# Expert FFN in one kernel: the first bank of block 0 by samples, other filler counts, block 0's second weight asked for by GpSimd, and block 1's order of work

## The reference

```
h = gelu(x @ Wi[e] + bi[e])            # 256 -> 1024, erf form
r = h @ Wo[e] + bo[e] + x              # 1024 -> 256
y = (r - mean(r)) * rsqrt(var(r) + 1e-12) * gamma[e] + beta[e]
```

## Time and profile before

| | us |
|---|---|
| median of 3 runs | 121.52 (121.5 to 121.61) |
| the profiled execution, its own time | 122.44 |
| its span, first to last instruction | 120.7 |
| TensorE busy in the span | 111.6 |
| DVE, ScalarE, GpSimd busy | 97.9, 94.6, 56.1 |
| mean granted TensorE clock | 0.974 |

### The profile page before, as it was taken

One profiled execution on the slowest core, in us unless ns is written; L12 is line 12 of the kernel. 1 busy time (PEld: TensorE's weight loads), 2 busy tenths in 40 slices (PEclk: granted clock), 3 DMA queues, 4 the chain that ended last, 5 costly groups with the idle time before them and its releaser, 6 DMA issues.

```text
span 120.7 us, 2768 instructions
## 1 busy us (share of the span) xinstructions
PE 111.6 (92%) x886; PEld 109.4 (91%) x886; DVE 97.9 (81%) x192; ACT 94.6 (78%) x187; POOL 56.1 (47%) x84
## 2 busy tenths in 40 slices
PE   5959999999999999999999999999999999999900
PEld 5848999999999999999999999999999999999800
DVE  2563079995979999999999999999999994975660
ACT  2261799798899999999999999999989929972100
POOL 5035001803647464652846375374724880493420
PEclk9995999999999999999999999999999999999995
DMA  2989999999999989987998899999930140011032
GB/s 63 291 265 326 349 395 395 387 400 392 383 384 376 360 268 328 379 271 200 375 380 234 268 329 312 234 356 312 309 132 5 46 120 16 3 49 43 11 81 57
DMA packets 21400, 29.82 MB, mean 247 GB/s; under 512 B 2368, under 2 KB 11584, under 8 KB 21376
## 3 DMA queue, kind: packets, MB, share of 16 engines
q1 hardware_dynamic: 19008, 24.89, 61.4%
q0 software_dynamic: 864, 2.36, 6.2%
q10 hardware_dynamic: 1504, 2.30, 6.0%
HBM read 27.19 MB, written 2.36 MB: 245 GB/s over the span
## 4 chain that ended last, share of the span: by engine, by line
PE 74%; DMA 9%; SPq 4%; DVE 4%; issue 3%; POOL 2%; ACT 0%; POOLq 0%; DVEq 0%
PE preact L834 12%; PE sums_ps L867 12%; PE preact L808 11%; PE preact L807 11%; PE sums_ps L808 11%; PE sums_ps L807 11%; DMA params<-vectors 7%; SPq L271 3%; PE preact L831 3%; DMA xT_in<-x_columns 2%; PE preact L787 2%; DVE h_lo L684 1%; POOL rstd L428 1%; DVE r L692 1%; POOL xs L418 1%
## 5 line engine op out<-in xcount | busy, mean ns | idle before, releaser
L834 PE MATMUL preact<-xT_r,wi_lo 128*128 128x256 f32 x140 | 40.0, 286 | 0.0
L807 PE MATMUL preact<-xT_r,wi_hi 128*128 128x256 f32 x140 | 39.5, 282 | 0.0
L808 PE MATMUL preact<-xT_r,wi_hi 128*128 128x256 f32 x140 | 39.4, 281 | 0.0
L867 PE MATMUL sums_ps<-wo_r,h_lo 128*128 128x256 f32 x136 | 38.6, 284 | 0.2 <-DVE h_lo L684 0.2
L807 PE MATMUL sums_ps<-wo_r,h_hi 128*128 128x256 f32 x136 | 38.3, 282 | 0.0
L808 PE MATMUL sums_ps<-wo_r,h_hi 128*128 128x256 f32 x136 | 38.2, 281 | 0.0
L283 POOL DMA_INDIRECT xs<-x_rows,row_of x18 | 19.9, 1107 | 18.9 <-DMA wi_in<-w_in 9.7
L834 PEld LDWEIGHTS preact<-xT_r,wi_lo 128*128 128x128 f32 x140 | 26.5, 189 | 0.1
L807 PEld LDWEIGHTS preact<-xT_r,wi_hi 128*128 128x128 f32 x140 | 26.5, 189 | 0.1
L808 PEld LDWEIGHTS preact<-xT_r,wi_hi 128*128 128x128 f32 x140 | 26.4, 188 | 0.0
L684 DVE TENSOR_TENSOR h_lo<-preact,h_hi 128x512 fp32r<-128x512 f32 x34 | 23.3, 686 | 3.8 <-ACT h_hi L538 3.7
(11 more groups left out here) (70 smaller groups left out, 107.5 us busy)
## 6 DMA issues: line engine op xcount, KB each, us to landing
wo_in<-w_out SPq DMA_DIRECT2D x8, 1024.0 KB
wi_in<-w_in SPq DMA_DIRECT2D x7, 1024.0 KB, 7.1
params<-vectors SPq DMA_DIRECT2D x9, 388.0 KB
y_rows<-xs SPq DMA_DIRECT2D x35, 64.0 KB
xT_in<-x_columns SPq DMA_DIRECT2D x34, 64.0 KB, 4.5
wi_in<-w_in ACTq DMA_DIRECT2D x2, 512.0 KB, 4.4
wo_in<-w_out ACTq DMA_DIRECT2D x2, 512.0 KB, 5.6
wi_in<-w_in SPq DMA_DIRECT2D x2, 512.0 KB, 7.0
```

The source lines that it names most:

```text
L807: nc.tensor.matmul(columns, weight, parts[:, 0, :], start=False, stop=False)
L808: return nc.tensor.matmul(columns, weight, parts[:, 1, :], start=False, stop=stop)
L834: nc.tensor.matmul(columns, wi_lo[:, t % 2, c, k, :], xT_r[:, t % 2, k, 0, :], start=(k == 0), stop=False)
L867: nc.tensor.matmul(columns, h_lo[:, t % 2, c, tokens], wo_r[:, t % 2, c, 0, :], start=(c == 0), stop=False)
```

## The change

- `WARM_UP` becomes (4, 6, 1), and one filler of 32 columns follows the first four.
- Two semaphores `first_x_loaded` take samples 0 and 2 of block 0's x apart from 1 and 3. Bank 0 of block 0's first product is computed for samples 0 and 2 first, then for 1 and 3: 128 columns at a time, in eight matmuls instead of four.
- Block 0's second weight is asked for by GpSimd, right after its constants, and no longer by ScalarE.
- DVE writes the rest of the table and the row numbers after `x_low(0)`, no longer before `wi_low(0, 0)`.
- GpSimd gathers block 0's rows once `wi_loaded[2]` is there, and block 1's once `wo_loaded[1]` is there. Before, the first went out as soon as the row numbers stood, the second after `wi_loaded[2]`.
- In iteration 1, ScalarE does `gelu` and `h_high` of bank 0 before `wo_high(1, 0)`, and bank 1's before `wo_high(1, 1)`; DVE likewise; DVE's `centre(0, 0)` and `centre(0, 1)` stand one place later; ScalarE's `deviations` of block 0 and GpSimd's `root(0, 0)` move to iteration 2; GpSimd's first residual waits for `wo_low(1, 0)` alone.
- A store's wait for `y_ready` is part of the transfer's instruction.

```diff
...
     WO_PIECES = [(0, IC // 2), (IC // 2, SPLIT_CHUNKS)]
-    WARM_UP = (5, 4, 2)
+    WARM_UP = (4, 6, 1)
...
         par_loaded = [sem(f"par_loaded{i}") for i in range(PAR_RING)]
+        first_x_loaded = [sem(f"first_x_loaded{i}") for i in range(2)]
         xT_loaded = [sem(f"xT_loaded{i}") for i in range(XT_RING)]
...
                               xt[bass.ds(rows[j], 1), :, :].rearrange("o p f -> (o p) f")).then_inc(
-                                  xT_loaded[t % XT_RING], 16)
+                                  first_x_loaded[j % 2] if t == 0 else xT_loaded[t % XT_RING], 16)
...
             for j in slots:
-                eng.wait_ge(y_ready, 2 * t + j // 2 + 1)
-                eng.dma_start(out[bass.ds(rows[j], 1), :, :].rearrange("o s h -> (o s) h"), slot(t, j)).then_inc(
-                    stored[t % X_RING], 16)
+                eng.dma_start(out[bass.ds(rows[j], 1), :, :].rearrange("o s h -> (o s) h"), slot(t, j)).wait_op(
+                    y_ready, 2 * t + j // 2 + 1, "sem-ge").then_inc(stored[t % X_RING], 16)
...
+            for i, (a, z) in enumerate([(0, IC // 2), (IC // 2, IC)]):
+                pool.dma_start(wo_in[:, 0, a:z, :].rearrange("p c h -> p (c h)"), wo[0, :, a * H:z * H],
+                               max_dma_last_dim=PIECE).then_inc(first_wo_loaded[i], 16)
             def residual(t, tile):
...
                 if t == 1:
+                    pool.wait_ge(wo_lo_done[0], 1)
+                    residual(0, 0)
                     pool.wait_ge(wo_lo_done[1], wo_lo_count(1, 1))
-                    residual(0, 0)
                     residual(0, 1)
-                    root(0, 0)
                 else:
+                    if t == 2:
+                        root(0, 0)
                     if ahead:
...
             pool.wait_ge(rows_ready, 2)
+            pool.wait_ge(wi_loaded[2], 16)
             load_x(pool, 0)
-            pool.wait_ge(wi_loaded[2], 16)
+            pool.wait_ge(wo_loaded[1], 16)
             load_x(pool, 1)
...
             load_xT(act, 0, (2, 3))
-            for i, (a, z) in enumerate([(0, IC // 2), (IC // 2, IC)]):
-                act.dma_start(wo_in[:, 0, a:z, :].rearrange("p c h -> p (c h)"), wo[0, :, a * H:z * H],
-                              max_dma_last_dim=PIECE).then_inc(first_wo_loaded[i], 16)
...
             def x_high(t):
-                act.wait_ge(xT_loaded[t % XT_RING], 4 * loads_of(t, XT_RING))
+                if t == 0:
+                    for pair in range(2):
+                        act.wait_ge(first_x_loaded[pair], 16 * QUAD // 2)
+                else:
+                    act.wait_ge(xT_loaded[t % XT_RING], 4 * (loads_of(t, XT_RING) - (16 if t % XT_RING == 0 else 0)))
                 if t >= 2:
...
                     wi_high(2, 1)
-                    wo_high(1, 0)
-                    wo_high(1, 1)
                     gelu(1, 0)
                     h_high(1, 0)
+                    wo_high(1, 0)
                     gelu(1, 1)
                     h_high(1, 1)
+                    wo_high(1, 1)
                     gelu(1, 2)
                     h_high(1, 2)
-                    deviations(0, 0)
                     gelu(1, 3)
                     h_high(1, 3)
-                    deviations(0, 1)
                     return
...
                     wi_high(t + 1, 0)
+                    if t == 2:
+                        deviations(0, 0)
                     x_high(t + 1)
+                    if t == 2:
+                        deviations(0, 1)
                 gelu(t, 0)
...
                                           slot_of[:, 0:1], None, ALU.is_equal))
-            dve.wait_ge(permuted, 2)
-            nc.vector.tensor_tensor(table[:, FIRST:T_ALL], later_ps[0:1, FIRST:T_ALL], table_base[:, FIRST:T_ALL],
-                                    ALU.add).then_inc(table_ready, 1)
-            dve.wait_ge(const_step, 9)
-            dve.wait_ge(spread, 1)
-            for half in range(2):
-                rows = slice(half * S, (half + 1) * S)
-                nc.vector.scalar_tensor_tensor(row_of[rows, :], tab_ps[rows, 256:256 + SLOTS].rearrange(
-                    "p (t h) -> p h t", h=2)[:, half, :], float(S), row_base[rows, :], ALU.mult, ALU.add).then_inc(rows_ready, 1)
             def wi_low(t, piece):
...
                     wi_low(2, 1)
+                    h_low(1, 0)
                     wo_low(1, 0)
+                    h_low(1, 1)
                     wo_low(1, 1)
-                    h_low(1, 0)
-                    h_low(1, 1)
+                    h_low(1, 2)
                     centre(0, 0)
-                    h_low(1, 2)
+                    h_low(1, 3)
                     centre(0, 1)
-                    h_low(1, 3)
                     return
...
             x_low(0)
+            dve.wait_ge(permuted, 2)
+            nc.vector.tensor_tensor(table[:, FIRST:T_ALL], later_ps[0:1, FIRST:T_ALL], table_base[:, FIRST:T_ALL],
+                                    ALU.add).then_inc(table_ready, 1)
+            dve.wait_ge(const_step, 9)
+            dve.wait_ge(spread, 1)
+            for half in range(2):
+                rows = slice(half * S, (half + 1) * S)
+                nc.vector.scalar_tensor_tensor(row_of[rows, :], tab_ps[rows, 256:256 + SLOTS].rearrange(
+                    "p (t h) -> p h t", h=2)[:, half, :], float(S), row_base[rows, :], ALU.mult, ALU.add).then_inc(rows_ready, 1)
             wi_low(0, 2)
...
         def _(pe):
-            def warm_up(count):
+            def warm_up(count, columns=P):
                 for _ in range(count):
-                    nc.tensor.matmul(preact[:, 0, 0:P], warm[:, :], warm[:, :], start=True, stop=True)
+                    nc.tensor.matmul(preact[:, 0, 0:columns], warm[:, :], warm[:, 0:columns], start=True, stop=True)
...
             warm_up(WARM_UP[0])
+            warm_up(1, P // 4)
             one = ones[:, 0:1]
...
                 raw = t == 0 and q == 0
-                if raw:
-                    pe.wait_ge(xT_loaded[0], 16 * QUAD)
-                elif q == 0 or t == 0 and q == 1:
+                if not raw and (q == 0 or t == 0 and q == 1):
                     pe.wait_ge(x_ready, t + 1)
...
                     pe.wait_ge(wi_lo_done, wi_count(t, piece))
+                if raw:
+                    for pair in range(2):
+                        pe.wait_ge(first_x_loaded[pair], 16 * QUAD // 2)
+                        for c in (2 * q, 2 * q + 1):
+                            columns = preact[:, q, (c % 2) * N:(c % 2 + 1) * N].rearrange("p (j s) -> p j s", j=QUAD)
+                            for k in range(HC):
+                                last = nc.tensor.matmul(columns[:, pair::2, :], wi_in[:, 0, c, k, :], xT_in[:, 0, pair::2, k, :],
+                                                        start=(k == 0), stop=(k == HC - 1))
+                    last.then_inc(preact_ready, 1)
+                    return
                 for c in (2 * q, 2 * q + 1):
...
                     for k in range(HC):
-                        if raw:
-                            last = nc.tensor.matmul(columns.rearrange("p (j s) -> p j s", j=QUAD), wi_in[:, 0, c, k, :],
-                                                    xT_in[:, 0, :, k, :], start=(k == 0), stop=(k == HC - 1))
-                            continue
                         nc.tensor.matmul(columns, wi_lo[:, t % 2, c, k, :], xT_r[:, t % 2, k, 0, :], start=(k == 0),
```

## The result

The changed kernel takes 124.14 us (median of 4, 123.8 to 124.84) beside 121.56: a ratio of 1.022, 95% interval 1.017 to 1.027. It is **2.2% slower**; 119.3 was forecast. On another chip (e8) the ratio was 1.011 (1.006 to 1.017). One kernel's executions spread much more than the 0.1 us said at the start: the kernel before ran from 120.38 to 123.09 in 29 executions on the last chip.

A forecast was written before the change was run, and what follows sets the result against it. Losses were placed before bank 1's start, at block 1's stall and after TensorE's end, with TensorE's stream otherwise closed. Gains 1.85 + 0.3 + 0.1 = 2.25 us, from 121.52, gave 119.3 us; range 118.8 to 121.6, forecast's own 118.8 to 120.2.

The forecast's parts named there:

- the term of GpSimd's request: Start: GpSimd's early request for block 0's second weight delays x by 0.4 us, with bounds of 0 and 1.3.
- pair 0: Samples 0 and 2 of block 0's x, forecast to land at 7.52 us, or 7.93 with the weight's delay.
- Rival 2: Start: the weight's packets push x to 9.0, where it meets a halved clock; 122.1 us, chance 0.12.
- the full clock over the first bank: Block 0's first bank runs at full clock, so bank 1 starts at 9.93 instead of 11.78, 1.85 us won.
- The fillers: Before the sort product: four and a quarter fillers for five bring product and x 0.15 us sooner; L798 at most 0.5 later.
- The bank's price: First bank as 16 records of 128 columns: 2.0 us at full clock, 4.0 at the halved one.
- The worth of the split: First bank by samples: the first pair starts at 7.93, ahead of the second at 8.48; no separate gain given.
- rival 1: First bank: the clock falls all the same, leaving 0.1 us won instead of 1.85; 121.0 us, chance 0.24.
- Block 1's order: Block 1: bank 0 before the second weight removes most of TensorE's 0.48 us wait for h_lo; 0.3 us won.
- the 1.85 us at the start: Start: bank 1 of block 0 begins at 9.93 instead of 11.78, counted as a separate gain in the sum.
- Table, gathers, stores, residuals: Later table costs 0; moved gathers leave residuals covered by 2 us or more; stores win 0.1 us.
- The stores' 0.1: End of the kernel: moving two register instructions before the store's wait wins 0.1 us of 0.17.

The follow-up runs named there:

- e8: The changed kernel itself, unaltered, measured again on another chip against the kernel before: ratio 1.011.
- e1: The changed kernel, but ScalarE asks for block 0's second weight after its two x issues, as before the change: 119.68 us, ratio 0.981.
- e5: The changed kernel, but GpSimd asks for the second weight only after the sort's last step on DVE: ratio 0.980.
- e4: The changed kernel, but GpSimd asks for the second weight only once all four samples of block 0's x are there: ratio 1.008.
- e11: The changed kernel with six full fillers instead of one after the sort's last product: ratio 1.003.
- e6: e1 with block 0's first bank computed whole, after all four samples of x: ratio 0.977.
- e3: The changed kernel, but GpSimd asks for only the first half of the second weight, ScalarE for the rest after its x issues: ratio 0.989.
- e9: The changed kernel with the whole start of the kernel before; block 1's order, the gathers' waits and the stores stay new: ratio 0.984.
- e10: e6 with the fillers of the kernel before, (5, 4, 2) and no short one: ratio 0.986.
- e15: The kernel before with only GpSimd's gathers of blocks 0 and 1 moved behind wi(2) and wo(1): ratio 0.996.
- e16: e9 with the gathers as in the kernel before, so block 1's new order and the stores alone: ratio 0.989.
- e12: e6 with three fillers instead of one after the sort's last product: ratio 0.984.
- e14: The kernel before, unaltered, profiled again on another chip: ratio 1.000.
- e13: e12 with block 1's order and the gathers as in the kernel before: ratio 1.001.
- e2: The kernel before with one part of the change, GpSimd asking for block 0's second weight right after its constants: 124.65 us, ratio 1.023.
- e7: The kernel before, but ScalarE asks for the second weight directly behind the first, ahead of the sort: ratio 1.020.

## Why the prediction was wrong, point by point

**The step that failed** is the term of GpSimd's request: "I take 0.4, nearer to the row of the same queue", with 1.3 us as the far bound. Without the request pair 0 was forecast at 7.52, and e1 has it at 7.42; with it, it came at 10.63 instead of 7.93. In the prediction's own terms the delay is 3.1 us (2.4 in e8). Three things were wrong in it. The gather's 4.6 us was read as a delay of GpSimd's queue; for the weight's own transfer that time goes by what was asked for before it (here 2.8, in e5 1.7), and the gather's, issued at 7.94 into full queues, may be of that kind too. Half of the megabyte was put into slack of the first nine microseconds as a mean, but the slack lies before 2.5 us, where hardly anything was asked for; from 3 us to x's landing the engines were 80% busy or more. And no row said that a transfer asked for earlier is served before a later one of another queue; I let them share. Rival 2 named the mechanism, x at 9.0, and 0.12 of the chance; x came at 10.63, and it gave 122.1. By the page's 1 us to the first byte, the sum would have been 120.2, nearer but wrong as well; e5's 1.7 is the nearest to it here, and the first byte is not what decides.

**A second term failed with it**, the full clock over the first bank: bank 1 was to start 2.0 us after pair 0 and started 4.53 after it. Of the 5.23 us between the forecast start, 9.93, and the measured 15.16, 2.70 are x's and 2.53 the pace's.

**The fillers**: the sort product came at 3.52 and x's issue 0.15 sooner. Right. L798 came 1.28 us later and not 0.5, since the six middle fillers ran at the slow pace; as forecast, nothing early read it.

**The bank's price**: 16 records at 0.125 and 0.25 a step; e4 and e11 show 2.02 in all, the changed kernel 3.75. Right. The worth of the split was wrong: e6 without it is no slower, and bank 1 starts 1.80 us after the first bank in e6, 1.87 and 1.78 in e4 and e5 with it.

**The clock**: rival 1 let it fall after a pause. That happened in e8; in the changed kernel's profile it had never risen, which the prediction did not consider, though it had read the first records as slow. The late x is not the only cause: the bank also ran slowly in e3, e9, e10, e15 and e16, with the first bank at 7.85 to 8.49, and at full pace in e11 with x at 9.87.

**Block 1's order**: 0.3 us was forecast. In the profile shown, the wait was 0.48 and is gone. But its real worth is what it lets through: the old order holds TensorE's end at 113.6 to 114.5 for starts of 9.7 to 11.8, so the 1.85 us at the start and the order are not two terms of a sum. That e1 and e12 came out near the forecast sum is in part luck: e9 has most of the gain, or all of it, without the start.

**Table, gathers, stores, residuals**: no cost shows, as forecast, though only the gathers were tried alone. The stores' 0.1 is not shown: TensorE's end to the span's end is 5.6 to 6.1 us with the new stores and 5.7 to 6.2 with the old ones (e14, before).

Without the early request the number of the forecast stands, if not its terms: e1's 119.68, e12's 119.25 (five of six executions between 119.05 and 119.44, one at 120.56). e6 (0.977) and e12 (0.984) beat both kernels.

## What to carry to other kernels

Ask for bytes in the order in which they are needed. A free engine is no reason to ask sooner: a megabyte that nobody needs for ten microseconds held back 256 KB that everybody waited for. Do not read the time from a request to its first packet as a delay of its queue before you have looked at what was asked for ahead of it. Before a gain at the start of a stream is counted, look for what it will run into: here a buffer released by work that stood behind a landing, so that the earlier start alone was worth nothing (e13, 1.001), while the new order with the stores, and the old start, was worth 1.1% (e16).

## What the runs showed of the hardware that was not expected

Transfers of different queues were served nearly in the order of the requests, and why is open. The weight asked for at 2.24 or 2.60 went before x asked for at 4.8, from GpSimd's queue as from ScalarE's (e2, e7, e8, the changed kernel), and x had next to no packet from 6 to 8 us; `first_bias`, which SyncE asked for at 2.46, moved only once block 0's first weight, asked for at 1.26, was nearly through, at 5.3. On SyncE's queue x also stood behind the small packets of `first_bias`; no run moved that request away, so what it costs x is open. GpSimd's direct transfer showed its first packets 1.7, 2.8 and over 4 us after the request, its gather 4.6. Two executions of one kernel, on different chips, put the first bank 0.4 to 0.7 us apart (8.28 and 7.86; 10.63 and 9.96), and its clock at either level. With the old order the end follows little of that: bank 1's starts of 11.78 and 9.74 gave TensorE's ends of 114.46 and 113.60, so close times are no proof of a steady start.
